# Splitting of expert weights moved to GpSimd, row pieces split one piece ahead, and a reordered turn in a decoder layer with alignment and routed experts

## The reference

```
x = x + attn(layernorm(x))        # gated linear scan over the 64 tokens, 3 projections, + its own input
x = x + align(ctx, layernorm(x))  # dynamic time warping of context against rows, per sequence
x = x + ffn(layernorm(x))         # one shared and 7 routed SwiGLU experts, hidden 352, top 1
```

## Time and profile before

| | |
|---|---|
| median of 3 runs | 336.13 us (336.00 to 337.49) |
| the profiled execution | 331.59 us, of which the span of instructions is 330.4 |
| mean granted TensorE clock | 0.924 |
| busy share of the span | PE 75%, DVE 62%, ACT 48%, POOL 47% |
| HBM traffic | 14.53 MB read, 8.50 MB written |

### The profile page before, as it was taken

How to read it: one execution, slowest core, us unless ns; L and a number is a source line. 1 busy time by engine, 2 the same in 40 slices (tenths; PEclk the granted TensorE clock), 3 DMA queues, 4 the chain that set the end, 5 groups by cost and what they waited for, 6 DMA issues and landing times.

```text
span 330.4 us, 5927 instructions
## 1 busy us (share of the span) xinstructions
PE 247.9 (75%) x1494; PEld 200.5 (61%) x1494; DVE 203.3 (62%) x827; ACT 159.9 (48%) x443; POOL 155.7 (47%) x229
## 2 busy tenths in 40 slices
PE   1185688966065286598898987877799999999993
PEld 1034366865032132387687866656599989899892
DVE  0579999770297998867787454647344444454451
ACT  1476577743575152689445231302155555454551
POOL 7366776647000000222176747063017676676677
PEclk9999999999659559989979779997999999999998
DMA  8999201223200000000012121143324345434431
GB/s 210 314 342 389 90 18 33 53 44 84 61 1 2 0 1 0 0 3 2 0 58 67 38 66 50 47 109 78 75 56 56 53 55 64 59 52 64 62 36 13
DMA packets 35664, 23.16 MB, mean 70 GB/s; under 512 B 8384, under 2 KB 32960, under 8 KB 35520
## 3 DMA queue, kind: packets, MB, share of 16 engines
q1 hardware_dynamic: 27720, 18.15, 19.9%
q0 software_dynamic: 6496, 4.24, 9.5%
q10 hardware_dynamic: 1416, 0.40, 0.6%
HBM read 14.53 MB, written 8.50 MB: 70 GB/s over the span
## 4 chain that ended last, share of the span: by engine, by line
PE 27%; issue 12%; DVE 9%; POOL 4%; DMA 4%; ACT 3%; SPq 1%; DVEq 0%; POOLq 0%; ACTq 0%
PE bank L857 6%; PE bank L766 4%; PE bank L768 4%; PE bank L1094 4%; PE bank L767 4%; POOL out L1163 3%; DMA out<-loan,xs 2%; DMA xs<-routed 2%; PE bank L1104 2%; DVE bn L163 1%; PE bank L721 1%; DVE xr L900 1%; PE bank L1065 1%; PE bank L776 1%; DVE xr L728 1%
## 5 line engine op out<-in xcount | busy, mean ns | idle before, releaser
L1163 POOL DMA_INDIRECT out<-loan,xs x38 | 58.8, 1548 | 44.0 <-DVE loan L1156 32.3
L172 POOL TENSOR_TENSOR rstds<-ve,half 128x4 f32<-128x4 f32 x24 | 27.7, 1154 | 44.8 <-DVE ve L170 40.0
L848 POOL DMA_INDIRECT routed<-pay,pos_i x32 | 31.9, 995 | 22.6 <-DVE fill_at L938 9.0
L873 ACT ACTIVATE loan<-bank 128x512 f32<-128x512 f32 (+1 forms) x24 | 14.2, 596 | 47.2 <-PE bank L768 24.1
L1094 PE MATMUL bank<-w_sb,h_ffn 128*128 (+1 forms) x228 | 33.3, 282 | 1.4 <-ACT h_ffn L1132 1.4
L1094 PEld LDWEIGHTS bank<-w_sb,h_ffn 128*128 128x128 f32 (+1 forms) x228 | 28.4, 191 | 3.7 <-issue 2.1
L1147 DVE TENSOR_TENSOR loan<-bank,loan 128x352 f32<-128x352 f32 x38 | 19.9, 525 | 17.1 <-ACT loan L1121 17.1
L766 PE MATMUL bank<-xT_hi,w_hi 128*128 128x512 f32 (+1 forms) x48 | 22.7, 472 | 9.3 <-issue 5.1
L1111 ACT CAST xs_hi<-bank 128x128 fp32r<-128x128 f32 x38 | 10.0, 267 | 40.1 <-PE bank L1094 26.7
L766 PE MATMUL bank<-w_hi,xs_hi 128*128 x76 | 27.7, 365 | 0.7 <-DVE xs_lo L1138 0.7
L1138 DVE TENSOR_TENSOR xs_lo<-bank,xs_hi 128x128 fp32r<-128x128 f32 x38 | 11.0, 291 | 25.8 <-ACT xs_hi L1111 15.4
(11 more groups left out here) (223 smaller groups left out, 671.0 us busy)
## 6 DMA issues: line engine op xcount, KB each, us to landing
w_sb<-in_w SPq DMA_DIRECT2D x8, 352.0 KB, 7.6
xs<-routed SPq DMA_DIRECT2D x38, 65.0 KB
xr<-in_x SPq DMA_DIRECT2D x8, 256.0 KB, 5.7
cn<-in_ctx SPq DMA_DIRECT2D x8, 256.0 KB, 6.1
cT<-in_ctxT SPq DMA_DIRECT2D x8, 256.0 KB, 6.0
out<-xr SPq DMA_DIRECT2D x8, 256.0 KB
w_sb<-in_w SPq DMA_DIRECT2D x8, 192.0 KB, 10.2
dist<-d SPq DMA_DIRECT2D x7, 128.0 KB, 2.0
```

The lines of the kernel that those rows point to most:

```text
L172: return pool_done(pool.tensor_tensor(rstds[:, k, s], ve[:, k, s], half[:, s], ALU.pow))
L848: pool.indirect_dma_start(routed, bass.IndirectOffsetOnAxis(ap=pos_i[:, n:n + 1], axis=0), pay[:, n, :], None, bounds_check=TABLE - 1).the ...
L1163: pool.indirect_dma_start(out_rows, bass.IndirectOffsetOnAxis(ap=xs[:, s % XB, ROW - 1:ROW].bitcast(U32), axis=0), y[:, s % 4, :], None, b ...
```

## The change

1. **Weights**: the rest of a piece is computed on POOL from SBUF (raw minus high, 128x512) right behind ACT's rounding; the two matmuls, ACT's second copy and `minus_r` go. Three pieces stand at steps 5, 7 and 9 of the recurrence, the other eight at steps 16 to 23, behind `gates(0)`. The walk back has none.
2. **Rows**: `split_rows` becomes `keep_high(c + 1)` (ACT, ahead of `up(c, 1)`) and `keep_rest(c + 1)` (DVE, ahead of `down_all`).
3. **First piece**: normalised on DVE instead of ACT, without the two small POOL operations; its high and rest are taken straight from the transposes' bank, and xT is copied after.
4. **Turn**: `align(turn + 1)` is written near the end of a turn instead of `align(turn)` at its start; in odd turns the first routing step comes ahead of the mask and `add_aligned`; the fillers of turns 0 and 1 change.
5. **Ring of tile rows**: XB is 12 instead of 8; the last store of x3 stays at tile 8.

```diff
-            def high_part(k):
...
-                pe_done(pe.matmul(o[:, :], ident[:, :], raw_flat[:, a], start=True, stop=False))
-                pe.wait_ge(*weights["hi", k])
-                weights["rest", k] = pe_done(pe.matmul(o[:, :], minus_r[:, :], hi_flat[:, a], start=False, stop=True))
...
-                weights["lo", k] = act_done(act.copy(lo_flat[:, k * CW:(k + 1) * CW], LOW[k % len(LOW)][:, :]))
+            def split_weights(k):
+
                 a = slice(k * CW, (k + 1) * CW)
-                after(act, *(m_w13[i] for i in e))
+                after(act, m_w13[k * CW // (2 * HID)], m_w13[((k + 1) * CW - 1) // (2 * HID)])
                 weights["hi", k] = act_done(act.copy(hi_flat[:, a], raw_flat[:, a]))
+                pool.wait_ge(*weights["hi", k])
+                weights["lo", k] = pool_done(pool.tensor_tensor(lo_flat[:, a], raw_flat[:, a], hi_flat[:, a].bitcast(F32), ALU.subtract))
...
-                if 4 <= i < 18:
-                    split_weights((i - 4) // 2, i % 2, 7)
                 if i in gates_at:
                     gates(gates_at[i])
+                if i in (5, 7, 9) or 16 <= i < 16 + splits - 3:
+                    split_weights((i - 5) // 2 if i < 16 else i - 13)
...
-                split_weights(7 + step // 2, step % 2, splits)
...
-        XB = 8
+        XB = 12
...
-            m = ln_stats(2, c, m)
+            m = mark("rstd", c, ln_stats(2, c, m))
+            if c == 0:
+                return
...
+            if c == 0:
+                dve.wait_ge(*old("rstd", c))
+                for t in range(CT):
+                    m = normalise(2, t, pay[:, t, 0:D])
+                mark("norm", c, m)
+                return
...
-            act.wait_ge(*old("turned", c))
+            if c == 0:
+                act.wait_ge(*old("turned", c))
+                m = mark("xT_hi", c, act_done(act.copy(xT_hi[:, 0:CW], X_T[:, :])))
+                dve.wait_ge(*m)
+                m = mark("split", c, dve_done(dve.tensor_tensor(xT_lo[:, 0:CW], X_T[:, :], xT_hi[:, 0:CW].bitcast(F32), ALU.subtract)))
+                act.wait_ge(*m)
+            after(act, old("turned", c))
...
+                if c + 1 < NC:
+                    keep_high(c + 1)
                 last, m_up = m_up, up(c, 1)
                 multiply(c, 0, *last)
+                if c + 1 < NC:
+                    keep_rest(c + 1)
...
-                if c + 1 < NC:
-                    split_rows(c + 1)
...
+        align(0)
         for turn in range(NC + 2):
...
+            if odd_turn:
+                step(here - 1)
             if turn + 1 < NC:
                 mask(turn + 1)
+            if turn == 1:
+                normed(0)
             if turn < NC:
-                align(turn)
                 add_aligned(turn)
-            if odd_turn:
-                step(here - 1)
-            else:
+            if not odd_turn:
                 step(here)
             put_rows(4)
-            if 1 <= turn <= NC:
+            if 2 <= turn <= NC:
                 normed(turn - 1)
             if turn >= 2:
                 next(expert)
-            else:
-                keep_busy(3)
             if turn + 2 < NC:
                 distance_to_middle(turn + 2)
+            if turn == 0:
+                keep_busy(4)
+            if turn == 1:
+                keep_busy(9)
...
+            if turn + 1 < NC:
+                align(turn + 1)
             if turn >= 3:
                 next(expert)
-            elif turn < 2:
-                keep_busy(3)
             step(here)
...
-                if s == XB:
+                if s == XB - 4:
                     store_x3(NC - 1)
```

More of the change, by code:

```diff
@@ L80, in program @@
         w13_sb = sb("w13_sb", [P, NE + 1, 2 * HID], at=early, side="right")
-        minus_r = sb("minus_r", [P, P], F32R)
         w2_sb = sb("w2_sb", [P, NE + 1, KC, D])
@@ L485, in program @@
             Wd = sb("Wd", [P, 2, 2, T], BF16, at=st)
-            act_done(act.mul(minus_r[:, :], ident[:, :], -1.0))
             fetch_table(ACT.Sqrt)
@@ L511, in program @@
             raw_flat = w13_sb[:, :, :].rearrange("p e h -> p (e h)")
-            LOW = [bank[k] for k in (2, 3, 4, 6, 7)]
+            splits = (NE + 1) * 2 * HID // CW
             weights = {}
-            def high_part(k):
-                e = (k * CW) // (2 * HID), ((k + 1) * CW - 1) // (2 * HID)
+            def split_weights(k):
                 a = slice(k * CW, (k + 1) * CW)
-                after(act, *(m_w13[i] for i in e))
+                after(act, m_w13[k * CW // (2 * HID)], m_w13[((k + 1) * CW - 1) // (2 * HID)])
                 weights["hi", k] = act_done(act.copy(hi_flat[:, a], raw_flat[:, a]))
-                o = LOW[k % len(LOW)]
-                after(pe, *(m_w13[i] for i in e), weights.get(("lo", k - len(LOW))))
-                pe_done(pe.matmul(o[:, :], ident[:, :], raw_flat[:, a], start=True, stop=False))
-                pe.wait_ge(*weights["hi", k])
-                weights["rest", k] = pe_done(pe.matmul(o[:, :], minus_r[:, :], hi_flat[:, a], start=False, stop=True))
-            def low_part(k):
-                act.wait_ge(*weights["rest", k])
-                weights["lo", k] = act_done(act.copy(lo_flat[:, k * CW:(k + 1) * CW], LOW[k % len(LOW)][:, :]))
[L532 to L539, removed]
+                pool.wait_ge(*weights["hi", k])
+                weights["lo", k] = pool_done(pool.tensor_tensor(lo_flat[:, a], raw_flat[:, a], hi_flat[:, a].bitcast(F32), ALU.subtract))
             def gates(k):
@@ L622, in program @@
                                                       accum_out=W[:, i:i + 1]))
-                step = HT2 - 1 - i
-                split_weights(7 + step // 2, step % 2, splits)
                 if i == 16:
@@ L750, in keep_turned, with keep_high, keep_rest @@
         def keep_turned(c):
-            act.wait_ge(*old("turned", c))
+            if c == 0:
[5 more added lines that the diff above has]
+            after(act, old("turned", c))
             mark("xT", c, act_done(act.copy(xT[:, c * CW:(c + 1) * CW], X_T[:, :])))
-        def split_rows(c):
+        def keep_high(c):
+            act.wait_ge(*old("xT", c))
+            mark("xT_hi", c, act_done(act.copy(xT_hi[:, c * CW:(c + 1) * CW], xT[:, c * CW:(c + 1) * CW])))
+        def keep_rest(c):
             a = slice(c * CW, (c + 1) * CW)
-            act.wait_ge(*old("xT", c))
-            m = act_done(act.copy(xT_hi[:, a], xT[:, a]))
-            dve.wait_ge(*m)
+            dve.wait_ge(*old("xT_hi", c))
             mark("split", c, dve_done(dve.tensor_tensor(xT_lo[:, a], xT[:, a], xT_hi[:, a].bitcast(F32), ALU.subtract)))
@@ L995, in program @@
                 keep_turned(turn - 1)
-                if turn == 1:
-                    split_rows(0)
             if turn >= 2:
                 logits(turn - 2)
[L1000 to L1005, removed]
+            if odd_turn and here >= 0:
+                routing[here] = route(here)
+            step(here)
+            if turn + 1 < NC:
+                align(turn + 1)
             if turn >= 3:
                 next(expert)
-            elif turn < 2:
-                keep_busy(3)
             step(here)
```

## The result

The kernel after takes 336.81 us (median of 20 runs, 335.11 to 338.66) where the kernel before took 336.02 (20 runs, 331.65 to 341.18): ratio 1.007, 95% interval 1.0039 to 1.0101. So after is slower by 0.2% by the medians and by 0.7% by the ratio, where I forecast 332.4 and faster. The profiled execution of after took 336.53 us with a span of 334.6, so it stands for the median, while the profiled one of before (331.59) is at the low end of its runs.

The account below looks back on a forecast made before the run. It took TensorE to bound the tiles and stage 3, and DVE's recurrence stage 2. Terms -2.3 + 11.0 + 0.5 - 0.5 - 9.0 - 5.1 + 2.2 - 0.5 = -3.7 took 336.13 to 332.4 us, range 320 to 340.

Parts of the forecast that it names:

- Rests on POOL: Stage 2: eleven POOL subtractions block DVE's recurrence through shared ports, 1.0 us each: +11.0, between 0 and 14.0.
- gate wait: Stage 2: DVE's 2.34 us wait for the gate, behind ACT's backlog of weight copies, goes: -2.3.
- fillers: End of the walk back: the 16 filler matmuls start at half clock, since TensorE no longer works before them: +0.5.
- No clash: Rival for stage 2: POOL's subtractions leave the recurrence at 0.60 us a step, giving 321.4; chance 0.23.
- Stage 3 by its own mechanism: Stage 3 gets 12.4 us shorter, to 95 instead of 107.4, through fewer TensorE waits and less low clock.
- the new wait for `multiply`: Stage 3: `multiply`, queued late on DVE, frees the banks of a later `up` late: one wait, +2.2 (0 to 8).
- the first piece's 0.5: First piece: DVE normalising and no xT copy ahead gain 1.6 us, later transposes give 1.1 back: -0.5.
- the four low-clock stretches: Stage 3: half-clock stretches after TensorE idling, 1.7 us each; three follow waits that go: -5.1.
- DVE takes over the turn: Rival for stage 3: in turns 4 to 8 TensorE waits for `multiply` queued on DVE, giving 339.9; chance 0.25.
- POOL's scatters start earlier with `pos`: Stage 3: the 32 scatters and the powers fit on POOL; no cost was charged.
- the wait of 3.96: Stage 3: TensorE's longest wait at a new piece; about 1.5 stays because of a late ACT activation, 2.46 goes.
- Twelve buffers: Tile stage: the larger row ring removes part of TensorE's 0.9 us wait for loaded rows: -0.5 (0 to -0.9).

Follow-up runs that it names:

- e2: Kernel before with only the new weight splitting (rests on POOL): 335.01 us, ratio 1.032.
- e4: Kernel after with 64 more small matmuls, which nobody reads, ahead of stage 3: 315.63 us, ratio 0.972, two runs.
- e1: Kernel after with the weights split as before, the rest of the change kept: 306.67 us, ratio 0.9435.
- e5: Kernel after unchanged, run again beside before in another job: 336.25 us, ratio 1.007.
- e7: Kernel after with the weights split as before, run in a job with stalls: 327.34 us, ratio 0.977.
- e16: Kernel after unchanged, run again in the last job, with stalls: 337.34 us, ratio 1.005.
- e12: Kernel before with a ring of 12 row buffers instead of 8, nothing else: 320.59 us, ratio 0.9864.
- e10: Kernel after with all stores of x3 moved into tiles 4 to 11 of SP's list: 316.28 us, ratio 0.975, two runs.
- e8: Kernel before unchanged, run and profiled again in a job with stalls: 336.04 us.
- e6: Kernel after with a ring of 8 row buffers instead of 12: 343.25 us.
- e11: Kernel after with weights split as before and at most three scatters per step of the shared expert, job without stalls: 309.94 us, ratio 0.955.
- e15: Kernel after with weights split as before and at most three scatters per step of the shared expert, job with stalls: 317.45 us, ratio 0.961.
- e14: Kernel after with all 32 scatters written behind the last turn of stage 3, job with stalls: 347.37 us, ratio 1.051.
- e18: Kernel after with all 32 scatters held back until the last mix of x3, job with stalls: 363.6 us.
- e9: Kernel after with all 32 scatters written behind the last turn of stage 3, job without stalls: 324.25 us, ratio 0.998.
- e17: Kernel after with only the pacing added, at most three scatters per step of the shared expert: 328.13 us, ratio 0.975.

## Why the prediction was wrong

*Rests on POOL, gate wait, fillers*: forecast -2.3 + 11.0 + 0.5 = +9.2; measured +9.2 (some 10 by the ratio), +9.0 and +8.9 (e2 against before, e4 against e1, e5 against e7). Right in mechanism and in size, and term by term in the first profile: -2.3, +11.6, and 0 for the fillers, whose 5.20 us end at 139.94, with Wd ready at 139.87; in e2, e4 and e16 they hold line 614 up by 0.6. "No clash" is out.

*Stage 3 by its own mechanism*: forecast 12.4 shorter; without stalls 13.4 (e12 against e10). Idle time fell by 9.6 (forecast 9.0 + 0.5 - 2.2 = 7.3), the clock brought 3.8 (forecast 5.1); the new wait for `multiply` of 2.2 did not come (the longest in e10 is 0.85). That the sum came so near is in part luck: the first piece's 0.5 was not won by the first `down_all`, and two of the four low-clock stretches of before (0.57 from 194 to 198 and from 225 to 229) are not there without stalls: in e12 the clock is 1.00 from 189.00 to 233.70. The rival "DVE takes over the turn" (339.9) ends nearer to the measured time than my sum, for the wrong reason: no profile shows that queue.

*The step that failed* is half a sentence: "POOL's scatters start earlier with `pos`; 32 of them and the powers fit", costed at nothing. That they fit is true. But with earlier positions the two streaks of eight became one of sixteen (190.7 to 210.2): in no profile with the order of before is a streak longer than eight, and with that of after, the scatters where the change has them, it is 16 in jobs with stalls and 24 in those without. In jobs with the condition such a streak holds TensorE, ACT and DVE from some ten microseconds on to about its end. Stage 3 with and without it: order of after 107.5 (the first profile) against 88.7, so 19 us; order of before 107.4 or 111.4 (e8, 131.7 to 243.1) against 102.1, so 5 to 9. The change gives back 10 to 14 of its 13.4. The clue stood in the earlier trace rows: of the wait of 3.96 I said that ACT's activation came late "for a reason of its own", and left the reason there. That wait stands at the end of a streak (216.2 to 226.3) and is itself a stall: without stalls (e12) the four waits at a new piece are 1.16 to 1.28 each. Its "issue" was a hint, not a sure sign, since in e8 the same wait, 6.89 there, is booked to DVE's line 761.

*Twelve buffers*: forecast -0.5; measured 5.3 over the tiles of after (e6), and 4.4 to 5.1 in all on before (e12). I took the idle rows as an upper bound. They aren't one: a transpose that comes late shows up in the step between two transposes and in who waits for it, of which the idle time in front of TensorE is only a part. This term is off by a factor of ten, and its error of 5 us has the sign opposite to the scatters': with eight buffers the kernel after takes 343.25 (e6, ratio 1.0255). The "busy 76.86 of 78.90" of the earlier trace rows misled me in the same way.

Together, without stalls: 9.2 - 13.4 - 5.1 = -9.3, and 325.8 - 9.3 = 316.5, where e4 and e10 have 315.6 and 316.3. With stalls in the recorded measurement: 9.7 (stages 1 and 2) + 0.1 - 5.6 = +4.2 between the two profiled spans (330.4 to 334.6); as before's profile is 4.4 below its median and after's is at its own, the medians differ by 0.8 alone.

**A version that beats both** is e1's: old splitting of the weights, everything else of the change, 0.9435 in a job without stalls and 0.977 in one with. With the scatters paced (e11, e15) it is 0.955 and 0.961: a little slower where nothing stalls, and safer where it does.

## What to carry to other kernels

Moving work to an idle engine is to be priced by the ports that it shares with the busy one: 11 hidden POOL operations cost DVE's recurrence 11.6 us, 9 with the gate wait that they replaced. An unexplained long wait in the trace of before ("issue", "remote") must be explained before the waits around it are priced, above all when the runs spread by 3%. And a background engine that is given its work earlier may bunch it: look at the longest uninterrupted streak, not only at whether the sum fits.

## What the runs showed of the hardware that I had not expected

In three of five jobs, and in the recorded measurement, an unbroken streak of indirect DMAs from POOL (one per 1.28 us, 16 or 24 of them) went with a TensorE that from about the tenth microsecond on started one matmul per 0.7 to 1.4 us for most of the time, while DVE stood still for up to 23.69 us (e14), 19 of them behind the start of the last matmul that it needed, and ACT for up to 22.94; with the scatters held back (e18) it did not happen; streaks of 8 cost 0 to 7 us at their end. In the other two jobs streaks of 24 and of 32 (e9) did nothing of the kind. Streaks of at most eight (e17) gave 9.2 us of 337.3 back. The same kernel before took 325.7 and 325.8 in the latter, 332.3 to 336.8 in the former.
